# Expert biases of the mixture stage: added by VectorE from broadcast rows, or by TensorE with a selector of ones

## The reference, cut to what matters

```
slots = einsum(xn, softmax over slots)                 # 1024 slots of 768
h  = gelu(slots @ w1[e] + b1[e])                       # per expert e: 32 x 768 by 768 x 384
eo = h @ w2[e] + b2[e]                                 # per expert e: 32 x 384 by 384 x 768
out = x + softmax over all 1024 slots @ eo             # 6250 x 1024 by 1024 x 768
```

## Time and profile before

| | us |
|---|---|
| median of 3 runs | 3303.42 (3299.69 to 3303.58) |
| the profiled execution | 3298.73 |
| its span | 3297.0 |
| PE busy | 3078.9 |
| VectorE busy | 1898.3 |
| ScalarE busy | 1155.6 |
| GpSimd busy | 1869.7 |

### The profile page before, as it was taken

One profiled execution on the slowest core, in us unless ns is written; L12 is line 12 of the kernel. 1 busy time (PEld: TensorE's weight loads), 2 busy tenths in 40 slices (PEclk: granted clock), 3 DMA queues, 4 the chain that ended last, 5 costly groups with the idle time before them and its releaser, 6 DMA issues. The chain is left out here.

```text
span 3297.0 us, 62639 instructions
## 1 busy us (share of the span) xinstructions
PE 3078.9 (93%) x21857; PEld 2070.2 (63%) x21857; DVE 1898.3 (58%) x3437; ACT 1155.6 (35%) x1578; POOL 1869.7 (57%) x1804
## 2 busy tenths in 40 slices
PE   3769999999999999789999999999999998689998
PEld 1347777878787878556666666666666653345665
DVE  7854545554444444277777777777777773102332
ACT  4842323233323232245444444444444441111000
POOL 3377777777777777377666666666666631100000
PEclk8989999999999999899999999999999999899999
DMA  8789999999999999599889998998999879998995
GB/s 310 271 320 372 335 340 332 340 337 331 339 335 340 339 341 331 184 336 348 309 308 311 308 310 309 309 310 307 309 309 311 309 250 338 315 327 230 268 229 141
DMA packets 344868, 1013.79 MB, mean 307 GB/s; under 512 B 147903, under 2 KB 157578, under 8 KB 335592
## 3 DMA queue, kind: packets, MB, share of 16 engines
q0 software_dynamic: 137376, 664.09, 57.5%
q1 hardware_dynamic: 195152, 312.01, 29.2%
q10 hardware_dynamic: 12040, 33.69, 3.2%
HBM read 873.96 MB, written 129.21 MB: 304 GB/s over the span
## 5 line engine op out<-in xcount | busy, mean ns | idle before, releaser
L1610 POOL DMA_INDIRECT xs<-table,idx x833 | 877.2, 1053 | 473.4 <-PE m_part L1787 277.1
L1065 POOL DMA_INDIRECT xs<-table,idx x833 | 899.1, 1079 | 306.8 <-issue 192.8
L1787 PE MATMUL m_part<-xs 128*128 128x512 f16 (+1 forms) x3332 | 585.6, 329 | 27.1 <-DMA xs<-table,idx 22.0
L1382 PE MATMUL a_part<-xs 128*128 128x512 f16 (+1 forms) x3332 | 591.3, 328 | 15.3 <-DMA xs<-table,idx 11.0
L1787 PEld LDWEIGHTS m_part<-xs 128*128 128x128 f16 x3332 | 417.8, 142 | 164.9 <-issue 43.3
L1382 PEld LDWEIGHTS a_part<-xs 128*128 128x128 f16 x3332 | 409.6, 142 | 135.2 <-issue 26.7
L1816 PE MATMUL m_ps_l<-xs,m_xT 128*128 128x512 f16 x1764 | 388.7, 379 | 0.4 <-issue 0.2
L1803 PE MATMUL m_ps_s<-dw_mem,xn_mem 128*128 128x512 f16 x1296 | 312.4, 381 | 3.1 <-DVE xs L1677 3.0
L1816 PEld LDWEIGHTS m_ps_l<-xs,m_xT 128*128 128x128 f16 x1764 | 172.0, 98 | 207.9 <-issue 1.5
L1332 PE MATMUL a_ps_o<-Ws,xs 128*128 128x512 f16 x1764 | 294.8, 326 | 1.3 <-ACT xs L1115 1.2
L1115 ACT ACTIVATE xs<-xs 128x128 f16<-128x128 f32 x294 | 88.6, 310 | 464.7 <-DVE xs L1266 460.4
(11 more groups left out here) (418 smaller groups left out, 3909.4 us busy)
## 6 DMA issues: line engine op xcount, KB each, us to landing
xs<-in_L_ffn_w_dram SPq DMA_DIRECT2D x64, 1152.0 KB, 10.3
xs<-table SPq DMA_DIRECT2D x98, 384.0 KB, 6.2
xs<-table,idx POOLq DMA_INDIRECT x1666, 5.8
cw_dram<-xs SPq DMA_DIRECT2D x49, 512.0 KB
table<-arena SPq DMA_DIRECT2D x49, 384.0 KB, 3.1
table<-xs SPq DMA_DIRECT2D x49, 384.0 KB, 4.7
xs<-x_pad SPq DMA_DIRECT2D x49, 384.0 KB, 6.1
x_dram<-xs SPq DMA_DIRECT2D x49, 384.0 KB, 5.5
```

The costliest lines, as they stand in the source:

```text
L1065: pool.indirect_dma_start(out=ring[:, t, :], out_offset=None, in_=table, in_offset=bass.IndirectOffsetOnAxis(ap=idx[:, k:k + 1], axis=0)). ...
L1382: mm = nc.tensor.matmul(part[:, bass.ds(to + a, z - a)], pick[:, i % 2, :, t], ring[:, n % RING, half * D + a:half * D + z], start=False, ...
L1610: pool.indirect_dma_start(out=ring[:, t, :], out_offset=None, in_=table, in_offset=bass.IndirectOffsetOnAxis(ap=idx[:, n:n + 1], axis=0)). ...
L1787: mm = nc.tensor.matmul(part[:, bass.ds(off + at, e - f)], pick[:, i % 2, :, t], ring[:, n % RING, half * D + f:half * D + e], start=False ...
```

## The change

The biases of all experts are loaded once, ahead of all products, as plain rows. For group g, half g // 4, the four rows of group g lie beside the four of group g + 4 (or g - 4) in eight partitions that begin at 32 x (g mod 4). 16 DMAs on GpSimd's queue, none of which waits, take the place of 64. Four copies on VectorE build `of_expert` in the last columns of `brow2`: for each row a block of 32 ones that selects its expert's partitions, zeros elsewhere. Four more instructions scale the rows of b1 by US x PS, so that they stand in the scale of the sum. PE then adds the bias with one more fp32 product (8 rows of contraction, 128 output partitions, 384 columns) into `ps_h`, and with two more (512 and 256 columns) into `ps_e`: ahead of the others, except for group 0's `ps_h`, where it comes last. `hidden_bias` goes; gelu reads `ps_h` with the scale and writes `hb`, and up_product(g) waits for gelu of the group before. `expert_out` becomes a copy. In `down_product` the selector products stand ahead of the waits for `back` and for w2. Besides this, `ident32` is written before `ones`.

```diff
--- before.py
+++ after.py
@@ -1920,16 +1920,15 @@
         ps_o = ctx.enter_context(nc.psum_tensor("e_po", [P, 2, 1024], F32))
         w1_in = (w1_head, [sem(f"w1_in{q}") for q in range(2 * G)])
         w2_in = (w2_head, [sem(f"w2_in{q}") for q in range(G)])
-        b1_in = [sem(f"b1_in{half}") for half in range(2)]
-        b2_in = [sem(f"b2_in{half}") for half in range(2)]
+        b1_in, b2_in, b1_r = sem("b1_in"), sem("b2_in"), sem("b1_r")
         cw_in = [sem(f"cw_in{q}") for q in range(RT)]
         x_in = [sem(f"x_in{q}") for q in range(RX)]
         p_in = [sem(f"p_in{q}") for q in range(RX)]
...
@@ -1960,15 +1959,10 @@
                 ob_of[k] = n_ob
                 n_ob += 1
 
-        def load_bias1(eng, g):
-            wait(eng, hb_r, g)
-            for q in range(G):
-                eng.dma_start(bias1[NS * q:NS * (q + 1), :], eb1[g * G + q:g * G + q + 1, :].to_broadcast([NS, H])).then_inc(b1_in[g // HG], 16)
-
-        def load_bias2(eng, g):
-            wait(eng, eo_r, g)
-            for q in range(G):
-                eng.dma_start(bias2[NS * q:NS * (q + 1), :], eb2[g * G + q:g * G + q + 1, :].to_broadcast([NS, D])).then_inc(b2_in[g // HG], 16)
+        of_expert = brow2[:, KC * P // 2:KC * P // 2 + 2 * P].rearrange("p (h n) -> p h n", h=2)
+
+        def bias_rows(g):
+            return slice(NS * (g % HG), NS * (g % HG) + 2 * G)
 
         def load_up(eng, g, qs):
             wait(eng, up, g - 1)
@@ -2038,15 +2032,17 @@
 
             @block.gpsimd
             def _(pool):
-                for g in range(NG):
-                    load_bias1(pool, g)
-                    load_bias2(pool, g)
+                for to, of, landed in ((bias1, eb1, b1_in), (bias2, eb2, b2_in)):
+                    for g in range(NG):
+                        at = bias_rows(g).start + G * (g // HG)
+                        pool.dma_start(to[at:at + G, :], of[g * G:(g + 1) * G, :]).then_inc(landed, 16)
 
             @block.scalar
             def _(act):
                 def gelu(g):
-                    act.wait_ge(hb_r, g + 1)
-                    nc.scalar.activation(hb[:, :], hb[:, :], ACT.Gelu).then_inc(act_r, 1)
+                    act.wait_ge(up, g + 1)
+                    wait(act, turned, g)
+                    nc.scalar.activation(hb[:, :], ps_h[:, 0:H], ACT.Gelu, scale=1.0 / (US * PS)).then_inc(act_r, 1)
 
                 def hidden(g):
                     act.wait_ge(turned, g + 1)
@@ -2096,21 +2092,14 @@
             @block.vector
             def _(v):
                 link = Chain(v, dve)
+                v.tensor_copy(ident32[:, :], ident16[:, :]).then_inc(ident_r, 1)
                 v.memset(ones[:, :], 1.0).then_inc(ones_r, 1)
-                v.tensor_copy(ident32[:, :], ident16[:, :]).then_inc(ident_r, 1)
-
-                def hidden_bias(g):
-                    v.wait_ge(up, g + 1)
-                    v.wait_ge(b1_in[g // HG], 16 * G * (g % HG + 1))
-                    wait(v, turned, g)
-                    v.scalar_tensor_tensor(hb[:, :], ps_h[:, 0:H], 1.0 / (US * PS), bias1[:, :], ALU.mult, ALU.add).then_inc(hb_r, 1)
 
                 def expert_out(g):
                     v.wait_ge(down, g + 1)
-                    v.wait_ge(b2_in[g // HG], 16 * G * (g % HG + 1))
                     if g >= HG:
                         v.wait_ge(e_lo, HK)
-                    v.tensor_tensor(eo[:, g % HK, :], ps_e[:, 0:D], bias2[:, :], ALU.add).then_inc(eo_r, 1)
+                    v.tensor_copy(eo[:, g % HK, :], ps_e[:, 0:D]).then_inc(eo_r, 1)
                     v.wait_ge(eo_r, g + 1)
                     v.tensor_reduce(mx4[:, g % HK:g % HK + 1], eo[:, g % HK, :], AX_X, ALU.max, apply_absolute_value=True).then_inc(mx_r, 1)
 
@@ -2138,10 +2127,16 @@
                     v.wait_ge(late_sum, c + 1)
                     v.tensor_tensor(slots[:, c, K // 2:K], slots[:, c, K // 2:K], ps_o[:, c % 2, 0:K // 2], ALU.add).then_inc(late_added, 1)
 
-                hidden_bias(0)
+                v.wait_ge(ident_r, 1)
                 for g in range(HG):
-                    if g + 1 < HG:
-                        hidden_bias(g + 1)
+                    r = bias_rows(g)
+                    v.tensor_copy(of_expert[r, :, :].rearrange("p h (q s) -> p (h q) s", s=NS),
+                                  ident32[r, r].unsqueeze(2).to_broadcast([2 * G, 2 * G, NS])).then_inc(b1_r, 1)
+                v.wait_ge(b1_in, 16 * NG)
+                for g in range(HG):
+                    r = bias_rows(g)
+                    v.tensor_scalar(bias1[r, :], bias1[r, :], US * PS, None, ALU.mult).then_inc(b1_r, 1)
+                for g in range(HG):
                     if g == 0:
                         expert_out(g)
                     for c in late_units.get(g, ()):
@@ -2154,8 +2149,6 @@
                 low(0)
                 for k in range(NU):
                     b, h = units[k]
-                    if k in up_at:
-                        hidden_bias(up_at[k])
                     if k in down_at:
                         expert_out(down_at[k])
                     if k == MAX_AT:
@@ -2190,7 +2183,9 @@
             @block.tensor
             def _(pe):
                 def up_product(g):
-                    wait(pe, hb_r, g)
+                    wait(pe, act_r, g)
+                    if g > 0:
+                        nc.tensor.matmul(ps_h[:, 0:H], of_expert[bias_rows(g), g // HG, :], bias1[bias_rows(g), :], start=True, stop=False, skip_group_check=True)
                     if g == HG:
                         pe.wait_ge(late_added, DC)
                     for q in range(G):
@@ -2198,7 +2193,11 @@
                     for c in range(DC):
                         for q in range(G):
                             mm = nc.tensor.matmul(ps_h[NS * q:NS * (q + 1), 0:H], slots[:, c, g * P + NS * q:g * P + NS * (q + 1)], w1s[g % 2][:, q, c, :],
-                                                  start=(c == 0), stop=(c == DC - 1))
+                                                  start=(c == 0 and g == 0), stop=(c == DC - 1 and g > 0), skip_group_check=True)
+                    if g == 0:
+                        pe.wait_ge(ident_r, 1)
+                        pe.wait_ge(b1_r, 2 * HG)
+                        mm = nc.tensor.matmul(ps_h[:, 0:H], of_expert[bias_rows(g), g // HG, :], bias1[bias_rows(g), :], start=False, stop=True, skip_group_check=True)
                     mm.then_inc(up, 1)
 
                 def turn(g):
@@ -2210,15 +2209,18 @@
                     mm.then_inc(turned, 1)
 
                 def down_product(g):
+                    pe.wait_ge(b2_in, 16 * NG)
+                    wait(pe, eo_r, g)
+                    for a, e in ((0, 512), (512, D)):
+                        nc.tensor.matmul(ps_e[:, a:e], of_expert[bias_rows(g), g // HG, :], bias2[bias_rows(g), a:e], start=True, stop=False, skip_group_check=True)
                     pe.wait_ge(back, g + 1)
-                    wait(pe, eo_r, g)
                     for q in range(G):
                         pe.wait_ge(w2_in[g // HG][q], 16 * (g % HG + 1))
                     for c in range(HC):
                         for a, e in ((0, 512), (512, D)):
                             for q in range(G):
                                 mm = nc.tensor.matmul(ps_e[NS * q:NS * (q + 1), a:e], hT[:, c * P + NS * q:c * P + NS * (q + 1)], w2s[:, q, c, a:e],
-                                                      start=(c == 0), stop=(c == HC - 1))
+                                                      start=False, stop=(c == HC - 1), skip_group_check=True)
                     mm.then_inc(down, 1)
 
                 def product(k):
```

More of the change, by code:

```diff
@@ L1929, in mixture @@
         stored = [sem(f"stored{q}") for q in range(RX)]
-        (ident_r, ones_r, up, hb_r, act_r, turned, back, down, eo_r, mx_r, maxed, across, topped, spread_out, scaled, e_hi, e_lo, prod,
+        (ident_r, ones_r, up, act_r, turned, back, down, eo_r, mx_r, maxed, across, topped, spread_out, scaled, e_hi, e_lo, prod,
          act_done, summed, dve_done, late_sum, late_added, dve) = (sem(n) for n in (
-             "ident_r", "ones_r", "up", "hb_r", "act_r", "turned", "back", "down", "eo_r", "mx_r", "maxed", "across", "topped", "spread_out", "scaled",
+             "ident_r", "ones_r", "up", "act_r", "turned", "back", "down", "eo_r", "mx_r", "maxed", "across", "topped", "spread_out", "scaled",
              "e_hi", "e_lo", "prod", "act_done", "summed", "dve_done", "late_sum", "late_added", "dve"))
```

## The result

The changed kernel takes 3281.33 us (median of 4 runs, 3278.9 to 3285.77) against 3302.64: a ratio of 0.9943, 95% interval 0.9931 to 0.9954, or 15 to 23 us faster.

A forecast was written before the change was run, and what follows sets the result against it. Bounds taken: w2 transfers on saturated DMA engines in the head, PE then DMA in the middle, PE in the tail. By down_product(6) -3.5, tail +1.9: -1.6 us from 3303.42, so 3301.8; range 3294 to 3312.

The forecast's parts named there:

- What goes from the DMA engines: Mixture stage: 64 broadcasts, 4.72 MB, leave the DMA engines, worth 1.6 us per group in the head, 1.8 in the middle.
- all the traffic pays: Rival, chance 0.20: DMA engines bound the middle from 2847 on, all bias traffic there pays and stalls collapse; 3295.4 us.
- The start: Group 0 of the mixture: waiting for eight loads, four scalings and a selector product ends it 3.2 us later, at 2754.8.
- The w2 chain: Head: whether the late start reaches the w2 transfers; only in part, with the products starting 1.8 us earlier.
- The stall is gone: Before down_product(1): PE and w2 meet, the 4.06 us stall vanishes, down_product(1) takes 4.1 instead of 5.77 us, ending +1.4.
- The next two transfers give 1.6 back each: Head, w2 transfers after down_product(1): each 1.6 us shorter, taking +1.4 to -1.8 at the start of the products.
- The middle: 2847.57 to 2958: PE adds 1.9 us, bias traffic gives 2.4 back, the 3.35 us stall goes; down_product(6) ends 3.5 earlier.
- The selector product: PE's added fp32 bias product, priced by columns at 0.64 us for H and 1.29 for D.
- the fourth case: Rival, chance 0.07: selector products on PE bare their weight loads, two or four of 0.19 us each; +1.4, 3304.8 us.
- expert_out: Copy out of PSUM replacing the addition in each group: no change, bounds 0.1 us either way at groups 0 and 3.
- The slower case: Rival, chance 0.18: the start's wait carries through the head and no traffic relief comes back; +8.5, 3311.9 us.

## Why the prediction was wrong

**What goes from the DMA engines: the step that failed.** I priced the broadcasts by their bytes, "1.6 us per group". Bytes account for about half (12 of 25 us). The rest was the rate to which they pulled everything else, 314 GB/s for ten us in the group measured above: 4.0 us with its bytes, where I had 1.6. Over seven groups that estimate gives 28 us, and the run without traffic gained 25. I had a mean of 367 GB/s for a stretch that held both rates, and took it for the rate of the engines. The rival "all the traffic pays" had the right sign at 3295.4, but the same price by bytes, and lies 14 us above the result.

I also left three waits for DMAs out when I read PE's timeline, though the transfers of w2 behind two of them stood in my chain. Besides the 4.06 us before down_product(1) the head held 5.54 before up_product(3), and these, before down_product(2) and (3):

```profile
2809.86 6.49 PE L2220 MATMUL e_pe<-xs,idx 128*32 128x512 f32 x48 [6.58 <-DMA xs<-in_L_ffn_w_dram]
...
2834.73 6.00 PE L2220 MATMUL e_pe<-xs,idx 128*32 128x512 f32 x48 [17.84 <-DMA xs<-in_L_ffn_w_dram]
```

They are 1.11, 3.59 and 11.38 us in the changed kernel. There the larger part of the head's relief lay, while the stall that I priced was the smallest of the four.

**The start** came out as forecast: I had 9.0 us from the stage's begin to the end of group 0, with 1.6 for the scalings and 1.0 for the product; measured 8.1, 1.52 and 0.88. That four-row loads issue no faster held (0.52 us each). The first gelu began 8.1 us after the stage's begin, where my 2754 to 2756 meant 8.2 to 10.2. The late end of group 0 held back the load of w1 for group 2 as I said: it was issued 8.1 us after the stage's begin instead of 5.8, and in the six us before it the DMA engines moved 13 to 20 GB/s. The slow clock in up_product(1) came too (5.70 us). down_product(0) ended 5.5 us late, counted from the stage's begin, in my 4.5 to 6.3.

**The w2 chain.** "The stall is gone" before down_product(1) held. "The next two transfers give 1.6 back each" did not: they gave 6.7 and 4.3 (12.72 and 12.56 instead of 19.39 and 16.87). Of the first, about half is that w1 for group 3 was still moving when it was issued: it landed 4.0 us after that issue before, 0.4 us now. down_product(1) ended 2.1 us late (I had 1.4), the products began 7.5 us early (I had 1.8).

**The middle.** I let PE lead up to 2885.93 and took back 2.4 us after it, and kept most of the 11.53 us stall. Both stalls are gone and PE is never idle. Of the 9.3 us of selector products there only 0.9 came back when they were left out, so nearly all had taken the place of waits. Group 7's, 2.3 us behind the last wait, are bare by their place, as I said; that group 4's were bare too is not shown.

**The selector product** was mis-sized: 0.84 and 1.48 us, not 0.64 and 1.29. The difference is 0.20 both times, the length of one weight load (184 ns), where the fourth case had two and four (1.02 and 2.05 us in all). That case is refuted as priced. Whether the 0.20 is the first load standing bare no run shows.

**expert_out** as a copy: 957 ns as before, so nothing, as said. **The slower case**, 3311.9 with nothing given back, has its nearest run in the traffic put back: 3299.44, with the costs of the change and two thirds of the bytes. That is 12 us below the case and no slower than the kernel before; one third of the relief was still in it, so the case's price stays untested.

## What to carry to other kernels

Where transfers share saturated DMA engines, do not price one by its bytes at a mean rate: read the rate in windows of 2 us while it moves and while it does not. Broadcasts into 32 neighbouring partitions cost 25 us here, more than twice their bytes; spread over all partitions the same loads cost 12, and plain rows with a selector on TensorE 5.5 (changed kernel against the one without traffic). Small work added to an engine that waits for the same transfers can be largely hidden by these waits: 18.6 us of it cost 5.6 here.

## What the runs showed that I had not expected

The DMA share does not tell: it reads 0.96 at 266 GB/s, 1.02 at 280 and 1.01 at 426. Work of 18.6 us on TensorE, the engine busy 94% of the time, was worth 5.6. And one DMA with the values of four took 29 us more of the kernel than the four.
